# Second attention of a two-layer hybrid model: causal mask added by VectorE at the row maxima, output bias added by TensorE

## The reference, cut to what matters

```python
def _L0_attn_b_ref(x, Wq, Wk, Wv, Wo, bo):
    ...                                     # H = 16 heads, HD = 8
    q, k, v = (proj(Wq), proj(Wk), proj(Wv))
    scores = jnp.einsum('bhqd,bhkd->bhqk', q, k)
    causal = jnp.triu(jnp.ones((n, n), dtype=bool), k=1)
    scores = jnp.where(causal, -jnp.inf, scores)
    attn = jax.nn.softmax(scores / np.sqrt(HD), axis=-1)
    ctx = jnp.einsum('bhqk,bhkd->bhqd', attn, v)
    ctx = ctx.transpose(0, 2, 1, 3).reshape(b, n, D)
    return ctx @ Wo.T + bo
```

## Time and profile before

| what | value |
|---|---|
| device time, median of 3 runs | 2860.97 us (2857.17 to 2865.35) |
| profiled execution: span, first to last instruction | 2539.0 us |
| TensorE busy | 1882.7 us (74%), 15915 matmuls |
| VectorE busy | 1646.5 us (65%) |
| ScalarE busy | 1109.0 us (44%) |
| GpSimd busy | 1266.1 us (50%) |
| mean granted TensorE clock | 0.845 of full |
| second attention | about 1149 to 2036 us of the span |

### The profile page before, as it was taken

One profiled execution on the slowest core, in us unless ns is written; L12 is line 12 of the kernel. 1 busy time (PEld: TensorE's weight loads), 2 busy tenths in 40 slices (PEclk: granted clock), 3 DMA queues, 4 the chain that ended last, 5 costly groups with the idle time before them and its releaser, 6 DMA issues. The chain is left out here.

```text
span 2539.0 us, 45627 instructions
## 1 busy us (share of the span) xinstructions
PE 1882.7 (74%) x15915; PEld 1075.4 (42%) x15915; DVE 1646.5 (65%) x4684; ACT 1109.0 (44%) x2069; POOL 1266.1 (50%) x1244
## 2 busy tenths in 40 slices
PE   6797887887888777873887888988798977884000
PEld 3355545545545555551333334443343355563000
DVE  5538478578568674476785687787887366376232
ACT  1155355444455355660445544444354546564000
POOL 0026127647657675773334431143053357577776
PEclk9899999989999899995787887889897878898555
DMA  9300000100101687874122213113021287786222
GB/s 371 156 1 4 1 1 17 35 21 13 35 25 44 254 301 243 259 252 119 41 79 57 64 28 84 32 52 95 20 61 58 95 298 243 232 283 195 60 60 56
DMA packets 134252, 275.69 MB, mean 109 GB/s; under 512 B 29644, under 2 KB 44620, under 8 KB 128124
## 3 DMA queue, kind: packets, MB, share of 16 engines
q1 hardware_dynamic: 101256, 205.60, 24.5%
q0 software_dynamic: 32768, 67.17, 9.1%
HBM read 146.34 MB, written 125.93 MB: 107 GB/s over the span
## 5 line engine op out<-in xcount | busy, mean ns | idle before, releaser
L1479 POOL DMA_INDIRECT slots_in<-g_xs,g_place x512 | 511.8, 1000 | 306.3 <-ACT b_pT L2564 154.6
L2564 ACT ACTIVATE b_pT<-b_psE 128x512 f32<-128x512 f32 (+3 forms) x768 | 328.5, 490 | 409.7 <-PE b_psE L2463 207.7
L2314 DVE TENSOR_REDUCE b_peak<-b_psM 128x1 f32<-128x512 f32 (+3 forms) x768 | 392.5, 551 | 126.3 <-PE b_psM L2446 86.1
L1506 POOL DMA_INDIRECT r_xs<-slots_out,g_place x336 | 332.1, 988 | 262.8 <-ACT b_pT L2564 175.1
L2443 PE MATMUL b_psM<-b_stacks 72*128 72x512 bf16 (+3 forms) x768 | 273.3, 387 | 59.5 <-DVE b_peak L2314 29.2
L2459 PE MATMUL b_psE<-b_stacks 75*128 75x512 bf16 (+3 forms) x768 | 245.0, 374 | 47.3 <-ACT b_pT L2564 45.5
L1506 POOL DMA_INDIRECT g_xs<-slots_out,g_place x176 | 171.8, 976 | 92.5 <-issue 51.2
L2443 PEld LDWEIGHTS b_psM<-b_stacks 72*128 72x128 bf16 x768 | 81.4, 108 | 251.6 <-DVE b_peak L2314 142.1
L2473 PE MATMUL b_psV<-b_pT,b_vb 128*32 128x512 f32 (+3 forms) x1536 | 187.7, 571 | 0.3 <-ACT b_pT L2564 0.3
L2081 DVE COPY m_staged_w<-wgd 128x192 f32 x512 | 107.4, 280 | 87.4 <-PE m_psY L1786 79.6
L2081 DVE COPY n_staged_w<-wgd 128x192 f32 x512 | 106.6, 279 | 82.9 <-PE n_psY L1786 71.4
(11 more groups left out here) (659 smaller groups left out, 4122.3 us busy)
## 6 DMA issues: line engine op xcount, KB each, us to landing
wgd<-in_w_gdT SPq DMA_DIRECT2D x20, 1536.0 KB, 9.0
slots_in<-g_xs SPq DMA_DIRECT2D x26, 1024.0 KB
m_rows<-slots_in SPq DMA_DIRECT2D x104, 256.0 KB
slots_out<-m_y SPq DMA_DIRECT2D x104, 256.0 KB
n_rows<-slots_in SPq DMA_DIRECT2D x104, 256.0 KB
slots_out<-n_y SPq DMA_DIRECT2D x104, 256.0 KB
b_stacks<-q_parts SPq DMA_DIRECT2D x48, 192.0 KB
b_stacks<-k_parts SPq DMA_DIRECT2D x48, 192.0 KB
```

Of the source, the lines that this page charges most:

```text
L1479: self.nc.gpsimd.indirect_dma_start(self.G.slots_in[self.h], bass.IndirectOffsetOnAxis(self.G.place[:, TPH * self.h + t, k:k + 1], 0), sel ...
L1506: self.nc.gpsimd.indirect_dma_start(self.rows(i)[:, k, :], None, self.G.slots_out[t // TPH], bass.IndirectOffsetOnAxis(self.G.place[:, t, ...
L2314: nc.vector.reduce_max(to, taking()[:, 0:size], AX.X).then_inc(m_taken, 1)
L2564: nc.scalar.activation(pT[:, e % KEPT, h, q0:HALF], psE[:, j % BANKS, q0:HALF], ACT.Exp, scale=SCALE).then_inc(e_taken, 1)
```

## The change

Where a maximum reaches the diagonal, TensorE leaves the mask product out, and VectorE's `reduce_max` becomes one `tensor_tensor_reduce`: it reads the PSUM bank and the last `size` columns of mask_strip (a bf16 tile of 128 x 512 in SBUF: zeros, with -1e30 above the diagonal of the last 128 columns), adds them, writes the sum back to the bank and the row maximum to `peak`. It starts from -1e30. Maxima that do not reach the diagonal stay as they were, and so do the mask products of `scores`. GpSimd builds the strip with one memset and one select more at the start.

The bias: bo becomes one row of 128 values on one partition, loaded by one small DMA. `project` loses its two additions of bo, and with them two places of the side work. In `finish` TensorE adds for each tile of 128 tokens a product of a row of ones with bo into the same PSUM region. To make room, column shares R.delta's memory in this stage, L556's throw-away result goes to the logits, and negr and bo share a tile.

```diff
--- before.py
+++ after.py
@@ -357,7 +357,9 @@
     R.picked = m.sbuf("picked", [P, TPB, EXPERTS], BF16) if picked is None else picked
     R.before = m.sbuf("before", [P, TPB + 1, EXPERTS], BF16) if before is None else before
     R.earlier, R.ones_bf = m.sbuf("earlier", [P, P], BF16), m.sbuf("ones_bf", [P, P], BF16)
-    R.column, R.extra, R.delta, R.more = (m.sbuf(n, [P, EXPERTS]) for n in ("column", "extra", "delta", "more"))
+    R.extra, R.delta, R.more = (m.sbuf(n, [P, EXPERTS]) for n in ("extra", "delta", "more"))
+    R.column = m.sbuf("column", [P, EXPERTS])[:] if by_scalar else R.delta[:]
+    R.compared = R.column if by_scalar else R.logits[:, 0, :]
     R.number, R.number_f = m.sbuf("number", [P, OWNERS], I32), m.sbuf("number_f", [P, OWNERS])
     R.ends = m.sbuf("ends", [P, 2, EXPERTS])
     R.share = m.sbuf("share", [1, EXPERTS], BF16)
@@ -429,7 +431,7 @@
 
     probs, logits, top, index, keys, at, total, inverse = R.probs, R.logits, R.top, R.index, R.keys, R.at, R.total, R.inverse
     key_i, expert_i, slot_i, low, picked, before, hs, hsig = R.key_i, R.expert_i, R.slot_i, R.low, R.picked, R.before, R.hs, R.hsig
-    column, extra, delta, more, number_f, ends, owner, older = R.column, R.extra, R.delta, R.more, R.number_f, R.ends, R.owner, R.older
+    compared_last, extra, delta, more, number_f, ends, owner, older = R.compared, R.extra, R.delta, R.more, R.number_f, R.ends, R.owner, R.older
     m_taken, bias = R.m_taken, R.bias
     resumed = last_part = p % BPH > 0
     h, first = p // BPH, TPB * (p % BPH)
@@ -552,7 +554,7 @@
         nc.vector.tensor_scalar(delta[:], delta[:], G.old_tiles[:], None, ALU.add)
         from_tile = older
     yield
-    for i, compared in enumerate((ends[:, 1 - turn, :], column[:])):
+    for i, compared in enumerate((ends[:, 1 - turn, :], compared_last)):
         nc.vector.tensor_scalar(compared, ends[:, turn, :], from_tile[:, i:i + 1], 0.0, ALU.is_le, ALU.add,
                                 accum_out=owner[:, i:i + 1])
     nc.vector.drain()
@@ -938,7 +940,7 @@
             if b:
                 ffn_on_gpsimd(nc, pool, G, F, N, p, B, scatters[(b - 2) // BPH] if b >= 2 else None)
                 nc.gpsimd.iota(R.number[:], [[P, OWNERS]], base=0, channel_multiplier=1)
-                nc.gpsimd.iota(R.column[:], [[1, EXPERTS]], base=0, channel_multiplier=0, allow_small_or_imprecise_dtypes=True)
+                nc.gpsimd.iota(R.column, [[1, EXPERTS]], base=0, channel_multiplier=0, allow_small_or_imprecise_dtypes=True)
                 nc.gpsimd.memset(R.ones_bf[:], 1.0).then_inc(made, 1)
                 pool.wait_ge(made, 1)
                 nc.gpsimd.affine_select(out=R.earlier[:], in_=R.ones_bf[:], compare_op=ALU.is_gt, fill=0.0, base=0,
@@ -2190,18 +2192,20 @@
         stacks = m.sbuf("stacks", [P, GB, 2, HG, SEQ], BF16, side="right")
         qS, kS = ([stacks[:, GB - 1 - g, i, :, :] for g in range(GB)] for i in range(2))
         ident_bf, mask_q = m.sbuf("ident_bf", [P, P], BF16), m.sbuf("mask_q", [P, P], BF16)
+        mask_strip = m.sbuf("mask_strip", [P, HALF], BF16)
         vb = m.sbuf("vb", [P, QT, HB, VW])
         pT = m.sbuf("pT", [P, KEPT, HG, HALF])
         peak = m.sbuf("peak", [P, HG, QT])
         peak2 = m.sbuf("peak2", [P, HG, QT // 2, 2])
         negp = m.sbuf("negp", [HG * QT, 2, 3, P], BF16)
-        negr = m.sbuf("negr", [HG * QT, P])
+        small = m.sbuf("small", [HG * QT + 1, P])
+        negr, bo = small[0:HG * QT, :], small[HG * QT:, :]
         ctxu = m.sbuf("ctxu", [P, 2, HALF])
         inv = m.sbuf("inv", [P, 4, HG])
         ctx = m.sbuf("ctx", [P, QT, HB, WB])
         ctxT = m.sbuf("ctxT", [P, SEQ])
         xn, xnT = m.sbuf("xn", [P, TPB, DM]), m.sbuf("xnT", [P, SEQ])
-        wq, wk, wv, wo, bo = (m.sbuf(n, [P, DM]) for n in ("wq", "wk", "wv", "wo", "bo"))
+        wq, wk, wv, wo = (m.sbuf(n, [P, DM]) for n in ("wq", "wk", "wv", "wo"))
         v = m.sbuf("v", [P, QT, HB, WB])
         parts = m.sbuf("parts", [P, 2, 3, SEQ], BF16)
         flat_xn = xn[:].rearrange("p t d -> p (t d)")
@@ -2276,11 +2280,6 @@
                         nc.vector.drain()
                         dve.sem_inc(v_taken, 1)
                     yield
-                for u in range(2):
-                    nc.vector.tensor_tensor(x[:, 4 * u:4 * u + 4, :], x[:, 4 * u:4 * u + 4, :],
-                                            bo[:].unsqueeze(1).to_broadcast([P, 4, DM]), ALU.add)
-                    yield
-                nc.vector.drain()
 
             def finish(b):
 
@@ -2311,7 +2310,11 @@
                 h, qt, kh = MAXIMA[k]
                 size = min(HALF, (qt + 1) * P - kh * HALF)
                 to = peak[:, h, qt:qt + 1] if qt < 4 else peak2[:, h, qt - 4, kh:kh + 1]
-                nc.vector.reduce_max(to, taking()[:, 0:size], AX.X).then_inc(m_taken, 1)
+                if (qt + 1) * P - kh * HALF <= HALF:
+                    ps = taking()[:, 0:size]
+                    nc.vector.tensor_tensor_reduce(ps, ps, mask_strip[:, HALF - size:HALF], 1.0, MASKED, ALU.add, ALU.max, to).then_inc(m_taken, 1)
+                else:
+                    nc.vector.reduce_max(to, taking()[:, 0:size], AX.X).then_inc(m_taken, 1)
 
             def peaks():
                 nc.vector.drain()
@@ -2322,11 +2325,11 @@
                 high, mid, tail = (negp[:, g % 2, i, :] for i in range(3))
                 nc.vector.tensor_scalar(high, turned, -1.0, None, ALU.mult)
                 nc.vector.drain()
-                nc.vector.scalar_tensor_tensor(negr[:], turned, -1.0, high, ALU.mult, ALU.subtract).then_inc(m_taken, 1)
-                nc.vector.drain()
-                nc.vector.tensor_copy(mid, negr[:])
-                nc.vector.drain()
-                nc.vector.tensor_tensor(tail, negr[:], mid, ALU.subtract).then_inc(split_ready, 1)
+                nc.vector.scalar_tensor_tensor(negr, turned, -1.0, high, ALU.mult, ALU.subtract).then_inc(m_taken, 1)
+                nc.vector.drain()
+                nc.vector.tensor_copy(mid, negr)
+                nc.vector.drain()
+                nc.vector.tensor_tensor(tail, negr, mid, ALU.subtract).then_inc(split_ready, 1)
 
             def context(g, half):
                 turned = taking().rearrange("p (t h w) -> p t h w", t=4, h=HG)
@@ -2422,8 +2425,9 @@
                     pe.wait_ge(ctxT_ready, QT // 2 * b + 2 * u + 2)
                     ps = use()
                     for t in range(4):
-                        last = nc.tensor.matmul(ps[:, t * DM:(t + 1) * DM], ctxT[:, (4 * u + t) * P:(4 * u + t + 1) * P], wo[:],
-                                                start=True, stop=True)
+                        nc.tensor.matmul(ps[:, t * DM:(t + 1) * DM], ctxT[:, (4 * u + t) * P:(4 * u + t + 1) * P], wo[:],
+                                         start=True, stop=False)
+                        last = nc.tensor.matmul(ps[:, t * DM:(t + 1) * DM], G.ones[HG * QT:HG * QT + 1, :], bo, start=False, stop=True)
                     last.then_inc(m_done, 1)
                     yield
 
@@ -2438,13 +2442,8 @@
             def maximum(g, k):
                 h, qt, kh = MAXIMA[k]
                 n = min(HALF, (qt + 1) * P - kh * HALF)
-                diagonal = (qt + 1) * P - kh * HALF <= HALF
-                ps = use()
-                last = nc.tensor.matmul(ps[:, 0:n], qS[g][0:STACK, h, qt * P:(qt + 1) * P],
-                                        kS[g][0:STACK, h, kh * HALF:kh * HALF + n], start=True, stop=not diagonal, skip_group_check=diagonal)
-                if diagonal:
-                    last = nc.tensor.matmul(ps[:, n - P:n], ident_bf[:], mask_q[:], start=False, stop=True, skip_group_check=True)
-                last.then_inc(m_done, 1)
+                nc.tensor.matmul(use()[:, 0:n], qS[g][0:STACK, h, qt * P:(qt + 1) * P],
+                                 kS[g][0:STACK, h, kh * HALF:kh * HALF + n], start=True, stop=True).then_inc(m_done, 1)
 
             def turn_maxima(n):
                 pe.wait_ge(peak_ready, n + 1)
@@ -2590,13 +2589,16 @@
                         left -= count
 
             nc.gpsimd.memset(mask_q[:], 0.0)
+            nc.gpsimd.memset(mask_strip[:], 0.0)
             nc.gpsimd.iota(R.number[:], [[P, OWNERS]], base=0, channel_multiplier=1)
-            nc.gpsimd.iota(R.column[:], [[1, EXPERTS]], base=0, channel_multiplier=0, allow_small_or_imprecise_dtypes=True)
+            nc.gpsimd.iota(R.column, [[1, EXPERTS]], base=0, channel_multiplier=0, allow_small_or_imprecise_dtypes=True)
             nc.gpsimd.memset(R.ones_bf[:], 1.0)
             nc.gpsimd.tensor_copy(ident_bf[:], G.ident[:]).then_inc(made, 1)
             pool.wait_ge(made, 1)
 
             nc.gpsimd.affine_select(out=mask_q[:], in_=mask_q[:], compare_op=ALU.is_ge, fill=MASKED, base=0,
+                                    pattern=[[-1, P]], channel_multiplier=1)
+            nc.gpsimd.affine_select(out=mask_strip[:, HALF - P:], in_=mask_strip[:, HALF - P:], compare_op=ALU.is_ge, fill=MASKED, base=0,
```

(2 more changed lines are left out.)

## The result

The changed kernel takes 2896.86 us (median of 4 runs, 2893.7 to 2904.73), the kernel before 2863.16 us beside it (2857.17 to 2871.29): a ratio of **1.0115 [1.0085, 1.0146]**, slower by some 33 us. The forecast was 2856 us and its range ended at 2884.

What follows compares the result with a forecast made beforehand. The prediction let TensorE pace six slots, VectorE six and the prelude, the expert gather three; -15.0 + 7.7 + 1.5 + 4.0 + 2.0 - 4.2 - 1.0 = -5.0 us against 2861 gave 2856 us, range 2838 to 2884.

Steps and rivals of the forecast that it cites:

- bias products: In `finish`, 8 products of 0.25 us per run: +4.0 us in slots 9 and 13, +2.0 at the stage's end.
- rival C: In the 288 us paced by TensorE, less work lowers its granted clock by 0.05: 2873 us, chance 0.10.
- slot 5: A slot read as paced by VectorE; the `finish` run at its start was counted as costing nothing.
- Mask products off, -15.0: In six slots paced by TensorE, 32 removed products a slot at 0.078 us save 15.0 us; elsewhere nothing.
- VectorE's slots: Slots 2, 5, 6 and 10 to 12, read as paced by VectorE, with a granted clock of 0.85 to 0.88.
- rival A: TensorE's saving from the removed mask products counts in every slot: sum -23 us, 2838 us, chance 0.33.
- VectorE's surplus, +7.7 and +1.5: Each masked maximum costs 0.04 us more: +7.7 us in six slots paced by VectorE, +1.5 in the prelude.
- Rival B: At the masked maxima, the accumulator read is serial, 0.14 us each, and VectorE becomes the bound: 2886 us, chance 0.20.
- Additions of bo, -4.2: In the projections, six of VectorE's eight removed additions save 0.7 us each, 4.2 us; the other end is 0.
- The start, -1.0: At the stage's first norm, bo as one row lands sooner, saving 1.0 us, between 0 and 1.5.

Runs made afterwards that it cites:

- c2: The changed kernel, unchanged, run again for a trace on one chip with the kernel before: ratio 1.015 to the kernel before.
- d1: The changed kernel without the bias product, bo left out, masked maxima kept: ratio 1.0031 to the kernel before.
- c3: The changed kernel with mask product and plain maximum put back, bias kept on TensorE: ratio 1.0134 to the kernel before.
- f1: The changed kernel with mask product and plain maximum put back and no bias at all: ratio 1.0022 to the kernel before.
- g1: The kernel before without VectorE's additions of bo, their two places in the side work kept: ratio 1.0001 to the kernel before.
- f3: The changed kernel without bias, with both TensorE's mask product and VectorE's masked maximum: ratio 1.0073 to the kernel before.
- g3_bias_rows: Bias on TensorE as 128-row products, zeros but for bo in the first row, maxima of the kernel before: ratio 1.0011 to the kernel before.
- c4: The changed kernel with plain maxima everywhere and no mask in the maxima, bias product kept: ratio 1.0121 to the kernel before.
- d2: The changed kernel with the bias product's single row from partition 0, bo left out: one execution, 2882.6 us, kernel before 2833.5.
- d3: The changed kernel with the bias product taking all 128 rows, adding 1 in place of bo: ratio 1.0062 to the kernel before.
- g2_share_rows: The kernel before with the routing's one-row product zero-padded to 128 rows, same result: ratio 0.9982 to the kernel before.

## Why the prediction was wrong, point by point

| term | forecast, us | measured, us |
|---|---|---|
| bias products | +6.0 | +34 (c2 - d1), +32 (c3 - f1) |
| mask products off, VectorE's masked maxima | -5.8 | +3, give or take 10 (d1 - f1) |
| additions of bo off, start earlier | -5.2 | +6, give or take 7 (f1); 0, give or take 6 (g1) |
| sum | -5.0 | +33 [+24, +42] |

The three terms as measured add up to +43, which is what the changed kernel lost in c2_after_again; the +33 of the last row is the result's own.

**The step that failed** is "TensorE gets 32 more products of 128 columns in float32, the shape of the output projection … 0.25". It took the price from the earlier trace rows, a row of products that all have 128 rows, and ruled that the shape was the same. The shape differs in the rows, 1 for 128, and that makes each product, and the one of the output projection behind it too, start late: 0.41 in place of 0.22 us at the full clock, 0.72 at the half clock. In slot 5, where I counted nothing, the stretch grew as well (3.6 to 8.4 us in c3). The evidence stood in the trace of before. The single-row product L716 of the routing starts 0.16 us after its neighbour, and that one 0.07 after its own. Looking for a row with one partition, as I looked for one with an accumulator, would have found it. It shows 0.1 us for each change of rows, and a bias product brings two: 0.2 x 32 = +6.4 us, and +2.0 for slot 5, which would have put the sum at +3, and the term's upper end well above. Even so it would have been short. Counted from the records, a bias product adds 205 + 214 + 200 + 213 - 2 x 112 = 0.61 us at the full clock and 350 + 376 + 346 + 374 - 2 x 213 = 1.02 us at the half clock: 20 to 33 us for 32, with the 28 of c3_bias_only between them. In float32 both records of both products come late, not only the first after a change.

**Mask products off, -15.0.** Wrong in size, and in the direction that rival C named. They returned 3 to 12 us in all slots, each give or take some 10. I wrote that a fall of more than 0.03 in the windows would outweigh the sum: it fell by 0.03 (0.79 to 0.76), and it rose by as much when they were doubled. The windows of one kernel don't show this, since slots differ in much else; the point against C, that VectorE's slots have no lower clock, was no evidence. C's price, though, was for a fall on top of the -15.0; what the runs show is rather that the fall takes most of it back, and the total stays near nothing.

That the saving was partly hidden by VectorE as well is likely but not shown. In before the loads of the maxima waited 151.0 us for VectorE's banks (L2443 for L2314, which makes all 768 maxima). In after VectorE makes them on two lines, L2315 and L2317, and the waits are 139.7 + 36.9 = 176.6 us (170.2 in c2_after_again):

```profile
PEld b_psM L2445 <- DVE b_peak L2315: 139.7, 195, 3.5
PEld b_psM L2445 <- DVE b_peak L2317: 36.9, 67, 1.7
DVE b_psM L2315 <- PE b_psM L2445: 81.8, 98, 7.2
```

The last row was 82.1 us behind the mask product in before. The two directions that the earlier trace rows showed are both still there: taking the mask product away did not remove VectorE's wait, it hangs on the scores product now. That counts against rival A.

The Trainium skill ("TensorE: Matmul & The Clock Gate", part 1) has the full rate as released by activity. The measured order agrees: 0.76, 0.79 and 0.82 with 4036, 4511 and 4986 records in the same 865 us. I had weighed that rule with a chance of 0.10 and by the wrong rows.

**VectorE's surplus, +7.7 and +1.5.** Right in kind: 22 ns hand-over for the 40 forecast, and the prelude, where VectorE paces, went from 29.50 to 30.30 us. The part I didn't have is the bank, which is held 68 to 107 ns longer. It can be what makes f3 dearer than the hand-over (512 x 0.022 = 11 us at the most, 14 give or take 10 measured), but no run separates the two. Rival B is out: the read lies beside the next instruction.

**Additions of bo, -4.2.** Wrong, the other end (0) held: g1.

**The start, -1.0.** The first norm's wait for the landing fell from 3.25 to 1.6 us:

```profile
1266.17 1.64 DVE L385 BATCH_NORM_STATS2 b_stats<-g_x 128x6 f32<-128x128 f32 x8 [1.61 <-DMA b_small<-in_bo]
```

From the stage's start to the first maximum it was 41.9 us before and 41.4 after: half of what I took.

**Range and chances.** Slower had 0.30, with rivals B and C, neither of which was the mechanism that did it. No bound of the range held the bias term: its ends were 0.25 and 0.28 us, since I took it for measured.

## What to carry to other kernels

Take the price of a product from a row with the same number of rows *and* the same neighbours; a single-row product between products of 128 rows makes both itself and its successor start late (0.1 us a record here), and zero-padding it to 128 rows removes that for the price of a small memset. Don't book TensorE work that is removed as time won before the granted clock after the edit is known: here 475 products fewer or more moved the clock by 0.03 and TensorE's busy time by only 4 us. Compare windows of two profiles only where they come from one chip. And compare the time of a profiled execution with its span: where they are far apart, or where no such time is given, ask for a second profile before building on stretches of the first.

## What the runs showed of the hardware that was not expected

- A change between 128 rows and 1 row holds TensorE up. Float32, 128 columns: 200 to 214 ns a record against 112 at the full clock, 343 to 376 against 213 at the half clock. 16-bit, 160 columns: 0.16 to 0.18 us against 0.07. It isn't any change of rows: products of 72 and 128 rows follow each other after 0.06 us in the earlier trace rows. Where between 1 and 72 rows it begins, no run tells. The weight load of the next product then starts together with its matmul; between products of 128 rows it starts one record ahead, as in g3_bias_rows, whose loads are these:

```profile
2208.61 0.30 PEld L2425 LDWEIGHTS b_psM<-b_wo,b_ctxT 128*128 128x128 f32 x2 [0.42 <-DVEq L2290]
2208.83 0.30 PEld L2427 LDWEIGHTS b_psM<-b_bo_rows,g_ones 128*128 128x128 f32 x2
```

and its matmuls:

```profile
2208.64 0.46 PE L2425 MATMUL b_psM<-b_wo,b_ctxT 128*128 128x128 f32 x2 [0.21 <-DVEq L2290]
2208.94 0.39 PE L2427 MATMUL b_psM<-b_bo_rows,g_ones 128*128 128x128 f32 x2
```

  L2427's load starts at 2208.83, 0.11 us before its matmul. The Trainium skill ("TensorE: Matmul & The Clock Gate", part 3, "The mechanism") has, in its list of what overlaps, a weight load overlap with running products only where the two use different strips of rows, though a sentence ahead of that list also allows it by a background weight buffer. Here loads overlap where the strips are the same, and don't where 128 rows and one alternate, in both places of the one row; the measurement decides.
- The place of the single row, partition 0 or 32, makes no difference: 200 to 214 ns in both.
- The stretches of alternating products also went with a lower clock: 0.50 to 0.99 in the changed kernel, c3, c4 and d2, where the same stretches of before, d3 and g3 had 1.00. In d2_row0 it fell within the last one: the records stood 205 ns apart at its start and 375 after the sixth. That the hold-up itself brings the fall is likely, but not shown: the last projection of g2_share_rows had 0.57 without any bias product, and no run holds the clock still.
- VectorE's custom operation with accumulator gives 141 ns to the read, against 0.08 us for the built-in form of the earlier trace rows, and the read lies beside the next instruction.
